# A three-layer graph network on one Trainium2 core: message records that begin at any row, 560 tiles for 592, and row numbers copied by GpSimd

## What is computed

```python
def _spmm(row, col, vals, x):
    msg = vals[:, None] * x[col]
    return jax.ops.segment_sum(msg, row, num_segments=N)

def _layer(x_prev, row, col, vals, W_a, b_a, W_b, b_b):
    h = _spmm(row, col, vals, x_prev)
    z = (h + x_prev) @ W_a.T + b_a + h * x_prev @ W_b.T + b_b
    return jnp.where(z >= 0, z, NEG_SLOPE * z)
x = emb[x_ids]
x1 = _layer(x, row, col, vals, W1_1, b1_1, W1_2, b1_2)
x2 = _layer(x1, ...)
x3 = _layer(x2, ...)
return jnp.concatenate((x, x1, x2, x3), axis=1)
```

## Time and profile before

| | us |
|---|---|
| median of 3 runs (8935.71 to 8948.48) | 8945.59 |
| the profiled execution | 8948.78 |
| its span in the trace | 8947.1 |
| setup, to the first matmul of stage A | 3016 |
| stage A, second layer | 755 |
| stage B, second layer, with what leads in and out | 1106 |
| last matmul of stage B (4890.7) to first of the next stage A (5005.55) | 115 |
| landing of a message store after its issue, median on the page | 3.2 |
| memory traffic: HBM read, written | 963 MB, 756 MB |

### The profile page before, as it was taken

How to read it: one execution, slowest core, us unless ns; L and a number is a source line. 1 busy time by engine, 2 the same in 40 slices (tenths; PEclk the granted TensorE clock), 3 DMA queues, 4 the chain that set the end, 5 groups by cost and what they waited for, 6 DMA issues and landing times.

```text
span 8947.1 us, 257893 instructions
## 1 busy us (share of the span) xinstructions
PE 7924.2 (89%) x84296; PEld 7333.9 (82%) x84297; DVE 7107.3 (79%) x10046; ACT 4558.1 (51%) x14210; POOL 5595.2 (63%) x3638
## 2 busy tenths in 40 slices
PE   5999986799995688899999788899999788899999
PEld 4777775577773588799999788799999788899999
DVE  8999988799996877777777777777777777777777
ACT  0999990799993366611112566511112566511112
POOL 4788774588783233388886233488885333488884
PEclk8999995899996799999999999999999999999999
DMA  2111111211119988888886588888886688888885
GB/s 78 7 7 7 7 7 38 34 7 7 7 7 30 155 309 312 302 282 287 286 286 247 209 309 307 301 284 286 286 286 224 235 307 310 297 284 287 287 286 200
DMA packets 1005688, 1721.41 MB, mean 192 GB/s; under 512 B 378356, under 2 KB 429624, under 8 KB 1004920
## 3 DMA queue, kind: packets, MB, share of 16 engines
q0 software_dynamic: 378656, 958.17, 35.5%
q1 hardware_dynamic: 499680, 753.27, 23.7%
q10 hardware_dynamic: 127224, 8.24, 3.6%
HBM read 963.06 MB, written 756.12 MB: 192 GB/s over the span
## 4 chain that ended last, share of the span: by engine, by line
PE 56%; DVE 5%; issue 3%; DMA 3%; ACT 1%; DVEq 1%; SPq 0%; POOL 0%; POOLq 0%; ACTq 0%
PE ps L980 37%; PE ps L971 17%; DMA messages<-work 2%; DVE work L1334 2%; DVE hT L1297 1%; PE ps L1008 1%; PE ps L988 1%; PE ps L1009 1%; DVE work L1347 1%; ACT work L745 1%; SPq L644 0%; DVEq L1355 0%; PE ps L998 0%; DVE work L1321 0%; DVE hT L1359 0%
## 5 line engine op out<-in xcount | busy, mean ns | idle before, releaser
L980 PE MATMUL ps<-work 128*128 128x125 f32 x28416 | 3281.9, 278 | 45.8 <-DVE work L1363 45.5
L980 PEld LDWEIGHTS ps<-work 128*128 128x128 f32 x28416 | 3240.4, 192 | 87.2 <-DVE work L1363 46.9
L571 POOL DMA_INDIRECT work<-messages,work x1776 | 2708.8, 1525 | 615.9 <-issue 608.4
L971 PE MATMUL ps<-xb,work 125*128 x10752 | 1909.2, 222 | 450.8 <-DVE work L1334 426.3
L1363 DVE TENSOR_TENSOR work<-work,iota_p 128x1000 f32<-128x1000 f32 x1776 | 2120.0, 1194 | 0.4
L556 POOL PARTITION_BROADCAST work<-work x672 | 890.8, 1326 | 1854.9 <-DMA work<-slot_cols 903.6
L745 ACT ACTIVATE work<-ps,work 128x128 f32<-128x128 f32 x5376 | 1537.1, 369 | 960.4 <-PE ps L971 918.0
L971 PE MATMUL ps<-hT,work 125*128 x10752 | 1904.4, 221 | 0.0
L971 PE MATMUL ps<-work 125*128 x10752 | 1898.5, 220 | 0.0
L763 ACT ACTIVATE work<-work 128x8 f32<-128x8 f32 x1776 | 534.4, 301 | 2675.5 <-DMA work<-messages,work 2675.5
L870 PEld LDWEIGHTS ps<-hT 128*128 128x128 f32 x12768 | 1484.0, 196 | 297.1 <-ACT stage L668 227.3
(11 more groups left out here) (212 smaller groups left out, 5680.8 us busy)
## 6 DMA issues: line engine op xcount, KB each, us to landing
messages<-work SPq DMA_DIRECT2D x2688, 256.0 KB, 3.2
work<-messages,work POOLq DMA_INDIRECT x1776, 5.9
out_x<-xb SPq DMA_DIRECT2D x150, 125.0 KB
sorted_edges<-stage,run_idx POOLq DMA_INDIRECT x798
work<-slot_cols SPq DMA_DIRECT2D x672, 4.0 KB
work<-lane_places SPq DMA_DIRECT2D x532, 5.2 KB, 2.1
out_x<-xb ACTq DMA_DIRECT2D x4, 1562.5 KB
sorted_edges<-hT SPq DMA_DIRECT2D x4, 908.0 KB
```

The lines of the kernel that those rows point to most:

```text
L571: pool.indirect_dma_start(out=ck[:, n, :, :].rearrange("p h x -> p (h x)"), out_offset=None, in_=flat, in_offset=bass.IndirectOffsetOnAxis ...
L971: last = t.matmul(ps[:, n % PR, j * D:(j + 1) * D], col_hot[:, at:at + P], piece[:, bass.ds(offs[n], D)], start=k == 0, stop=k == 2)
L980: last = t.matmul(part[n], ck[:, n, j // CH, j % CH * D:(j % CH + 1) * D], sel[:, n % SELB, j, :], start=j == 0, stop=j == CHB - 1)
```

## The change

1. A message is now a record of its own, ROWF = 129 numbers: 128 columns and the row number. A tile's partition fetches 8 records beginning at any record, still 4128 bytes. TB falls from 592 to 560.
2. The row numbers are no longer stored by line 722. They are transposed (28 TensorE transposes) and kept as 16-bit integers in `row_of` (7 Scalar copies) in the setup. In stage A, GpSimd copies for each pair of groups 2 x 4 row numbers per partition into the record buffers (`put_rows`, 448 copies in a layer), after both buffers' stores have landed; SP waits for `rows_put` before it stores a pair, and counts a new semaphore that nobody waits for. The column broadcasts go two batches (8 groups) ahead of the copies, and GpSimd waits after each for its own result. SP stores 128 x 2064 bytes.
3. `group_at` holds four block numbers in each word. TensorE's loop holds LB = 4 bodies (64 groups) and loads 16 words; the block's offset is shifted, masked and multiplied in registers for each group.

```diff
-TB = -(-((E + (2 * (CH - 1) + CH) * NB * NB) // CHB // P + 1 + NB) // (2 * BU)) * 2 * BU
+ROWF = D + 1
+TB = -(-((E + (CHB - 1) * NB * NB) // CHB // P + 1 + NB) // (2 * BU)) * 2 * BU
...
-        messages = dram("messages", [CHUNKS + CHB // CH, CH * D + CH])
+        messages = dram("messages", [SLOTS2 + CHB, ROWF])
...
+                def put_rows(i, n, first):
+                    for k in (n, n + 1):
+                        if k >= MR:
+                            pool.wait_ge(msg_stored[k % MR], ...)
+                        elif not first:
+                            pool.wait_ge(msg_stored[k % MR], ...)
+                    taken_up()
+                    g.tensor_copy(msg[:, n % MR:n % MR + 2, :, D],
+                                  row_of[:, bass.ds(i * (AU * CH) + n * CH, 2 * CH)].rearrange("p (n j) -> p n j", j=CH)).then_inc(rows_put, 1)
+
+                def spread_cols(i, h, first):
+                    pool.wait_ge(col_src_in[h], ...)
+                    if not first or h >= CR2:
+                        pool.wait_ge(col_hot_ready, ...)
+                    if not first or h >= 3:
+                        pool.wait_ge(rows_put, la * (GROUPS // 2) + i * (AU // 2) + (h - 2) * (BATCH // 2))
+                    taken_up()
+                    g.partition_broadcast(col_row[:, h % CR2, :], col_src[h * 32:h * 32 + 1, :], channels=P).then_inc(col_spread[h], 1)
+                    pool.wait_ge(col_spread[h], la * ABODIES + i + 1)
+
+                def spread_body(i, first, last):
                     for h in range(CB):
+                        if h + CR2 < CB:
+                            spread_cols(i, h + CR2, first)
+                        elif not last:
+                            spread_cols(i + 1, h + CR2 - CB, False)
+                        for n in range(h * BATCH, (h + 1) * BATCH, 2):
+                            put_rows(i, n, first)
...
+                        if n % 2 == 0:
+                            sp.wait_ge(rows_put, la * (GROUPS // 2) + i * (AU // 2) + (n // 2 + 1))
+                            sp.sem_inc(stores_begun, 1)
                         sp.wait_ge(msg_ready[n % 2], ...)
-                        sp.dma_start(messages[bass.ds(i * (AU * P) + n * P, P), 0:CH * D], msg[:, n % MR, :]).then_inc(msg_stored[n % MR], DMA)
+                        sp.dma_start(records[bass.ds(i * (AU * P) + n * P, P), :], msg[:, n % MR, :, :].rearrange("p j e -> p (j e)")).then_inc(msg_stored[n % MR], DMA)
...
-            act.wait_ge(rows_found, 1)
-            act.dma_start(messages[0:CHUNKS, CH * D:REC].rearrange("(p c) j -> p c j", p=DP), slot_row).then_inc(slots_stored, DMA)
...
-                with pe.Fori(0, ABODIES) as i:
-                    _, offs = nc.values_load_multi_w_load_instructions(
-                        group_at[0:1, bass.ds(i * AU, AU)], engines=[mybir.EngineType.PE], ...)
-                    for n in range(AU):
+                with pe.Fori(0, ABODIES // LB) as i:
+                    _, four = nc.values_load_multi_w_load_instructions(
+                        group_at[0:1, bass.ds(i * (LB * AU // 4), LB * AU // 4)], engines=[mybir.EngineType.PE], ...)
+                    for n in range(LB * AU):
+                        offset = ((four[n // 4] >> (n % 4 * 8)) & 255) * D
...
-                                                piece[:, bass.ds(offs[n], D)], start=k == 0, stop=k == 2)
+                                                piece[:, bass.ds(offset, D)], start=k == 0, stop=k == 2)
...
-                            last = t.matmul(part[n], ck[:, n, j // CH, j % CH * D:(j % CH + 1) * D], sel[:, n % SELB, j, :],
+                            last = t.matmul(part[n], ck[:, n, j, 0:D], sel[:, n % SELB, j, :],
                                             start=j == 0, stop=j == CHB - 1)
...
-                dve.wait_ge(slots_stored, DMA)
+                dve.wait_ge(rows_kept, GPP)
```

More of the change, by code:

```diff
@@ L21 @@
 I32 = mybir.dt.int32
+I16 = mybir.dt.int16
 U8 = mybir.dt.uint8
@@ L546, in _ @@
                     gather_rows(NB // 2, NB)
-            flat = messages.rearrange("c (u e) -> (c u) e", e=CH)
             with pool.Fori(0, LAYERS) as la:
-                def spread_cols(i, first):
-                    for h in range(CB):
[L552 to L560, removed]
+                def put_rows(i, n, first):
+                    for k in (n, n + 1):
+                        if k >= MR:
+                            pool.wait_ge(msg_stored[k % MR], la * (GROUPS // MR * DMA) + i * (AU // MR * DMA) + (k // MR) * DMA)
+                        elif not first:
+                            pool.wait_ge(msg_stored[k % MR], la * (GROUPS // MR * DMA) + i * (AU // MR * DMA))
+                    taken_up()
+                    g.tensor_copy(msg[:, n % MR:n % MR + 2, :, D],
+                                  row_of[:, bass.ds(i * (AU * CH) + n * CH, 2 * CH)].rearrange("p (n j) -> p n j", j=CH)).then_inc(rows_put, 1)
@@ new lines, in spread_body @@
+                def spread_body(i, first, last):
+                    for h in range(CB):
+                        if h + CR2 < CB:
[4 more added lines that the diff above has]
+                            put_rows(i, n, first)
+                pool.wait_ge(rows_kept, GPP)
+                for h in range(CR2):
+                    spread_cols(0, h, True)
@@ L561, in _ @@
+                spread_body(0, True, False)
+                with pool.Fori(1, ABODIES - 1) as i:
+                    spread_body(i, False, False)
+                spread_body(ABODIES - 1, False, True)
                 for n in range(MR):
                     pool.wait_ge(msg_stored[n], la * (GROUPS // MR * DMA) + GROUPS // MR * DMA)
-                pool.wait_ge(slots_stored, DMA)
                 taken_up()
@@ L727, in _ @@
             act.wait_ge(vals_kept, GPP)
+            for k in range(GPP):
+                act.wait_ge(rows_turned, k + 1)
+                s.activation(row_of.rearrange("p (t k j) -> p k j t", k=GPP, j=CH)[:, k, :, :],
+                             ps[:, k, 0:CH * DP].rearrange("p (j t) -> p j t", j=CH), ACT.Copy).then_inc(rows_kept, 1)
+            act.wait_ge(rows_kept, GPP)
             with act.Fori(0, LAYERS) as la:
@@ L924, in _ @@
                 last.then_inc(vals_turned, 1)
+            pe.wait_ge(rows_found, 1)
+            for k in range(GPP):
+                pe.wait_ge(vals_kept, k + 1)
+                for j in range(CH):
+                    last = t.transpose(ps[:, k, j * DP:(j + 1) * DP],
+                                       slot_row[:, k * GE:(k + 1) * GE].rearrange("p (m j) -> p j m", j=CH)[:, j, :], ident[:, :])
+                last.then_inc(rows_turned, 1)
             when_asked()
```

116 lines of the change are left out of this document (65 added, 51 removed).

## The result

The changed kernel takes 8899.87 us (median of 5 runs, 8889.35 to 8903.36) against 8945.59 us of the kernel before: ratio 0.9946, 95% interval 0.9933 to 0.996. It is faster by 46 us, where 285 were forecast and the range began at 96.

The account below looks back on a forecast made before the run. TensorE was taken to bound stage B, and SP's queue stage A after the change. 8948.8 - 177.4 (tiles) - 81 (stage A) - 26 (setup) = 8664, about 8661 us against the median; range 8530 to 8850.

Parts of the forecast that it names:

- Fewer tiles: Stage B, paced by TensorE: 96 fewer tiles at 1.848 us each, a gain of 177.4 us, all on the path.
- Setup: Setup before the layers: 17 us less wait at line 1282, 5.9 us fewer steps, some 3 us shorter tables; together 26 us.
- Register loads, shift and mask: Stage A, TensorE: fewer loads give up to 92 us per layer; unpacking costs 0 to 1.6 us a body, taken as 0.
- The long loop: Stage A, TensorE's 64-group loop: branch or fetch costs 0 to 0.85 us a body, at worst 12.65 us a body.
- SP's queue: Stage A: new instructions add 1.4 us, 11.53 becomes 12.9 us a body; SP-bound at 13.0, gaining 81 us.
- DMA: Stage A's stores grow by 16 in 2048 bytes: 11.5 us a body becomes 11.6, below 13.0.
- Row copies: Stage A, GpSimd: 8 copies a body at 0.3 us; with broadcasts 7.7 us and some waits in 13, covered.
- the ring's rival: Stage A: store, landing and copy overrun 8 groups, so it stays at 13.5 to 14.2 us a body, 8745 to 8863; chance 0.18.

## Why the prediction was wrong

*Fewer tiles*: right. 177.4 us were forecast; stage B got 3 x 57 = 171 shorter, at 1.853 us a tile for 1.848. Runs that begin at any row of 516 bytes cost the gathers nothing: share 0.84 as before, GpSimd 1.53 us each.

*Setup*: right, 32.5 us for 26. The wait of line 1282 shrank by 17.2 us (forecast 17), the steps by 5.9 (5.9); the rest, 9 us, was more than the 3 of the tables.

*Register loads, shift and mask*: right as prices. A load of 4 words takes 0.6 us and the unpacking hides: between turns TensorE still makes a group in 0.68 us.

*The long loop*: this step failed, twice. The trace gave both ends, 0 and 3.4 us a turn, and I took 0; the branch took 4.2. The Trainium skill ("Runtime: NRT & Kernel Launch", Instruction fetch mechanics) would let 2048 instructions stay; here some 950 a turn stayed and about 1,900 did not, so a count near that figure was no safe sign. It doesn't refute the figure: at the 256 instructions that the same section gives a block of 16 KB, 9.5 packets a turn would be an estimated 2,400, and the trace doesn't say whether the fetch runs past the loop's end or the records miss instructions. The second fault is worse, because it made the first look harmless. I spread the branch over four bodies, 0.85 us each, got 12.65 for TensorE and compared it with SyncE's 12.9, so that even the bad end would have cost nothing. But four pauses of 2.2 us are not one of 6. PSUM and the message ring are 8 groups deep, some 6 us; in one long pause they run empty (the DMA share behind it is 0.25), and the 33 to 53 matmuls behind it run at half clock, which I had put at nothing for the new loop. Afterwards TensorE at 0.68 us a group is soon held by the ring again, and makes up for most of the pause but not all. Measured: 50 us a layer in the changed kernel, 69 with the packed numbers alone (785 - 716). Here the pause, the half clock and the slower issues on SyncE add up. Of the 239 us between forecast and result, the long loop is 174.

*SP's queue*, which I called the most important term: the price was nearly right (12.2 us a body of own work for 12.9), the role was wrong. The instructions alone cost nothing, and moved off SyncE they gave nothing. SyncE becomes the bound only with half the bytes.

*DMA*: wrong, and this step failed whatever the loop's length: with the short loops the kernel takes 8725 us for the forecast 8661, most of it here. I divided the share by itself, 11.5 us a body at a share of 1, and added 0.8% for the bytes. The stage stops well short of a share of 1. With stores of 2048 bytes a partition it settles at 12.8 us a body and a share of 0.89, with 2064 bytes at 13.4 and 0.87: 0.6 us for the 0.1 that I had put down. The run with half the bytes shows that it is the stores. What stops the share there is open. One reading is the ring: a store that lands later holds its buffer longer, and there are 8. The trace bears out that the ring has no slack. But in six kernels with stores of 2064 bytes and a short loop the share is 0.86 or 0.87 and the stage 745 to 757 us, while the landing goes from 3.9 to 5.2 us. A limit in the stores' own rate, with the landing as the queue in front of it, fits these numbers at least as well. A larger ring would tell the two apart and wasn't tried.

*Row copies*: right in size, 207 ns for 300, and GpSimd never became the bound. Some 8 to 11 us a layer with the short loop (745 against 753.5 and 756), and 16 with the long one. Vector's comparison takes 852 ns with copies (loop of 16) and 610 without, 242 more for a copy of 202; the Trainium skill ("SBUF — State Buffer", Who interferes with whom) says that GpSimd and VectorE in one of its 2-port modes exclude each other for an instruction's length, and the trace agrees in size.

Stage A of the second layer, step by step from run to run: 762 before; 716 with the packed numbers in a short loop; 749 with stores of 2064 bytes; 745 with the new order of the broadcasts and the layout of records; 756 with the copies; 805.5 with the long loop. Taken in another order the steps may differ, as the long loop's 69 us with the packed numbers alone shows. The 13.48 us a body that I started from left out the first 10.5 us of the stage; from first to last matmul it was 13.6.

*The rivals*: the ring's rival came nearest by its mechanism: landings of 4.0 us (4.8 in the short loop), the branch, restarts at half speed. Its 13.5 to 14.2 us a body (8745 to 8863) were too few: 14.4 and 8900. I had it at 0.18 because I measured it against a landing of 3.2 us, which was the landing of a stage with slack.

## What to carry to other kernels

Ask how long one pause is against what the buffers behind it hold, not what it is on average. Here a pause of about the ring's 6 us, every 64 groups, cost the stage 2.6 us each time without fetches and 3.7 with them, against the loop of 32; shared out over four bodies it had looked free. Unroll only as far as the loop stays loaded, and look for it in two rows, the branch at the head and the packets of the instruction queue; here the loops of 16 and of 32 groups were equally fast. A DMA share below 1 is not yet slack: here the stage stopped at 0.87 to 0.89, and each buffer was written again as soon as its store had landed. And a landing time read from a stage that waits for something else, 3.2 us here, says little of the landing once that wait is gone, 4.9.

## What was not expected of the hardware

While a long loop is fetched at every turn, SyncE's own DMA issues become slower on average (425 to 449 ns for 339), in the whole turn and not only beside the branch, in all three kernels with the long loop and in none of the others. The long ones overlap an instruction packet (98 of 98 in the changed kernel, 118 of 124 and 113 of 120 in the other two) and end 0.37 us after it. And 16 bytes more in a packet of 2048 cost 4.5% of the stage (749 for 716 us): landing rose by 0.3 us while the DMA engines were less busy.
